# One block of a language model on one core: attention prepared without a barrier, group weights one sequence behind the other

## The reference

```
tok = wte[x];  Q = layernorm(tok) @ W_proj.T;  V = tok @ W_val.T         # 8 heads of 64
traces = decay * (value_traces - erase(Q masked)) + lr * (Q masked)^T V / denom
h = Q shifted by one token @ traces @ W_out.T
x1 = layernorm(h)
q, k, v = x1 @ W_qkv + b_qkv
gw = softmax(gelu(v @ W_gp))                                             # 49 groups a token
group = gw @ gw.T
w = (1 - a) * softmax(q @ k.T * scale * group) + a * group               # a = sigmoid(alpha)
h = h + (w @ v) @ W_proj + b_proj
x2 = layernorm(h)
D, C = softmax over tokens, softmax over slots, of x2 @ phi_n            # 64 experts x 16 slots
h = h + C @ experts(D^T x2)                                              # layernorm, gelu, two layers
```

## Time and profile before

| | us |
|---|---|
| median of 3 runs | 500.75 |
| profiled execution | 499.41 |
| its span | 497.6 |
| PE busy | 450.2 |
| DVE busy | 305.7 |
| ACT busy | 215.2 |
| POOL busy | 145.4 |

### The profile page before, as it was taken

How to read it: one execution, slowest core, us unless ns; L and a number is a source line. 1 busy time by engine, 2 the same in 40 slices (tenths; PEclk the granted TensorE clock), 3 DMA queues, 4 the chain that set the end, 5 groups by cost and what they waited for, 6 DMA issues and landing times.

```text
span 497.6 us, 8397 instructions
## 1 busy us (share of the span) xinstructions
PE 450.2 (90%) x3098; PEld 364.8 (73%) x3098; DVE 305.7 (61%) x829; ACT 215.2 (43%) x398; POOL 145.4 (29%) x235
## 2 busy tenths in 40 slices
PE   5599999799669999999999899999649599999996
PEld 2387756797558888888888788899525387777785
DVE  4689853585844756767775857668522154455475
ACT  2387641399524336644224848163661212112220
POOL 4887400373100262210003930034211221223110
PEclk9999998899879999999999999999978979999999
DMA  8111000003000000400000000027057999997104
GB/s 295 45 42 34 1 2 0 0 2 109 16 0 0 1 1 9 183 1 0 1 0 2 2 0 2 0 88 295 0 200 302 386 345 405 387 375 275 31 27 126
DMA packets 14200, 49.65 MB, mean 100 GB/s; under 512 B 3472, under 2 KB 8496, under 8 KB 9936
## 3 DMA queue, kind: packets, MB, share of 16 engines
q1 hardware_dynamic: 6992, 41.64, 22.0%
q10 hardware_dynamic: 4256, 4.10, 2.4%
q0 software_dynamic: 2912, 3.37, 2.4%
HBM read 45.94 MB, written 3.15 MB: 99 GB/s over the span
## 4 chain that ended last, share of the span: by engine, by line
PE 75%; DVE 7%; ACT 6%; DMA 5%; POOL 4%; issue 3%; ACTq 0%; POOLq 0%; DVEq 0%
PE ps L1053 10%; PE ps L864 9%; PE ps L910 6%; PE ps L1005 4%; PE ps L1030 3%; PE ps L846 2%; PE ps L1041 2%; PE ps L677 2%; DMA ys<-ys_dram 2%; PE ps L890 2%; ACT ec L1271 2%; PE ps L819 2%; PE ps L582 2%; PE ps L893 1%; PE ps L891 1%
## 5 line engine op out<-in xcount | busy, mean ns | idle before, releaser
L1053 PE MATMUL ps<-ys,ct 128*128 128x192 f32 x256 | 52.0, 357 | 5.1 <-DMA ys<-ys_dram 5.1
L1793 DVE SCALAR_TENSOR_TENSOR res<-ps,riC,res 128x192 f32<-128x192 f32 x128 | 46.7, 413 | 12.1 <-PE ps L1053 9.6
L1053 PEld LDWEIGHTS ps<-ys,ct 128*128 128x128 f32 x256 | 41.5, 197 | 15.0 <-issue 8.5
L864 PE MATMUL ps<-pr,et 128*128 128x192 f32 x256 | 46.4, 332 | 2.1 <-DVE et L1641 1.6
L864 PEld LDWEIGHTS ps<-pr,et 128*128 128x128 f32 x256 | 41.1, 189 | 5.2 <-ACT et L1249 3.1
L485 POOL TENSOR_SCALAR ve<-mv 128x1 f32<-128x1 f32 x32 | 12.9, 403 | 103.5 <-DVE mv L1656 61.4
L1354 ACT ACTIVATE hs<-ps 128x384 f32<-128x384 f32 x16 | 7.9, 491 | 79.9 <-PE ps L1005 79.9
L570 POOL DMA_DIRECT2D ys<-ys_dram x32 | 19.7, 619 | 73.9 <-DMA ys_dram<-ysb 68.1
L1238 ACT ACTIVATE scs<-ps,pr 128x1024 f32<-128x1024 f32 x16 | 17.9, 1117 | 41.1 <-PE ps L823 41.1
L1784 DVE COPY ysb<-ps 128x192 f32<-128x192 f32 x16 | 5.7, 358 | 46.8 <-PE ps L1030 46.8
L1242 ACT ACTIVATE zz<-zz,nmx 128x1024 f32<-128x1024 f32 x16 | 18.4, 1150 | 26.4 <-DVE nmx L1635 26.3
(11 more groups left out here) (323 smaller groups left out, 1197.6 us busy)
## 6 DMA issues: line engine op xcount, KB each, us to landing
w1r<-in_p_w SPq DMA_DIRECT2D x16, 1152.0 KB, 11.8
w2r<-in_p_w SPq DMA_DIRECT2D x16, 1152.0 KB, 9.2
ys_dram<-ysb ACTq DMA_DIRECT2D x16, 96.0 KB, 7.7
ys<-ys_dram POOLq DMA_DIRECT2D x32, 48.0 KB, 6.9
phT<-in_p_phi SPq DMA_DIRECT2D x1, 1024.0 KB, 4.8
wT<-in_p_qkv ACTq DMA_DIRECT2D x1, 774.0 KB
out<-res SPq DMA_DIRECT2D x4, 192.0 KB, 3.2
out<-res ACTq DMA_DIRECT2D x4, 192.0 KB, 3.9
```

The lines of the kernel that those rows point to most:

```text
L864: last = mm(d[:, 0:D], et[:, k, :], pr[:, b * KT + k, 0:D], start=(k == 0), stop=(k == KT - 1))
L1053: mm(bank(5 + q % 3)[:, 0:D], ct[:, u % 2, k, :], ys[:, t % YR, b, :], start=True, stop=True).then_inc(m["yp_filled"], 1)
L1793: v.scalar_tensor_tensor(res[:, i, :], bank(5 + q % 3)[:, 0:D], riC[:, i:i + 1], res[:, i, :], ALU.mult, ALU.add).then_inc(m["yp_taken"], 1)
```

## The change

It has these parts:

- The first barrier is gone from all five engines; the waits on tile counts that are needed in its place are added. The tiles in SBUF are laid out in another order, so that what is loaded or written early lies on nothing still in use.
- The loads of wT, wpg, wvT, vt, woT and wpn move to SP's queue, behind the statistics of tile 1. phT and lnT load after the first mixed tile, the other two constants after the last value projection. GpSimd gathers three tiles instead of four ahead of the first factors, and factors 1 and 2 come ahead of gather 4.
- ScalarE loads its first table with a one-element Copy, and the Gelu table with a one-element Gelu, ahead of where they are first needed.
- The beta products of the four head pairs move from the start to right ahead of kB2, where VectorE copies them.
- The key bias is one more column of the k preparations and lies in column 0 of pr; four small products, bks and its scaling go.
- The order of SETUP is now beta, kA, kB1, kB2, nB2, nB1, nA, vA, vB1, vB2. The v preparations run inside the mixed/value loop, in steps 0, 1 and 3.
- The last gram products run right after the first loop's last steps, ahead of the update.
- Gelu, shift, Exp and normalising run for one sequence at a time, those of sequence 0 in part inside the mixed/value loop. scores(0) wait for the transposed group weights of sequence 0 only; sums and transposes of sequence 1 run in step 1 of attention, ahead of turn(0).
- Square and sum of phi are one step later.

```diff
@@ SyncE
+            sp.wait_ge(m["front_stats"], 2)
+            sp.dma_start(wT[:], a["p_qkv"]).then_inc(m["in_attn"], 16)
+            sp.dma_start(wpg[:], a["p_wpg"]).then_inc(m["in_attn"], 16)
...
-            meet(sp, 1)
+            sp.wait_ge(m["h_filled"], 1)
             sp.dma_start(phT[:], a["p_phi"]).then_inc(m["in_phi"], 16)
@@ GpSimd
-            for g in range(4):
+            for g in range(3):
                 gather(g)
             front_factors(0, 1)
+            gather(3)
+            front_factors(1, 3)
             gather(4)
-            front_factors(1, 3)
...
-            meet(pool, 1)
             nc.gpsimd.memset(gw[:], 0.0).then_inc(m["half_ready"], 1)
@@ TensorE, set-up
-            prepare("kB2", at["kA"] + 1)
+            prepare("kA", 1)
...
-            grams(NT - 1)
-            prepare("vA", 0)
...
-            prepare("vB1", at["kB2"] + 1)
+            prepare("kB1", 0)
...
-            prepare("vB2", at["vA"] + 1)
+            pe.wait_ge(m["setup_taken"], at["kA"] + 1)
+            beta_of_pairs()
+            prepare("kB2", at["kA"] + 1)
             pe.wait_ge(m["mm_ready"], 2)
+            pe.wait_ge(m["setup_taken"], at["kB2"] + 1)
@@ TensorE, mixed/value loop and attention
                 if s < NT:
                     mixed(s)
+                if s == 0:
+                    prepare("vA", 0)
+                if s == 1:
+                    prepare("vB1", 0)
                 if 3 <= s < NT + 3:
                     x1_T(s - 3)
+                if s == 3:
+                    prepare("vB2", at["vA"] + 1)
...
-            meet(pe, 1)
+            for j in range(2 * QPS - 2):        # QPS = 4 query blocks a sequence
+                query(j)
+            for j in range(GTS):                # GTS = 2 blocks of gw a sequence
+                gw_T(j)
+            for j in range(2 * QPS - 2, 2 * QPS):
+                query(j)
...
-                if s == 0:
-                    beside_scores()
+                if s == 1:
+                    sums(0)
+                    for j in range(GTS, NB * GTS):
+                        gw_T(j)
+                    sums(1)
@@ ScalarE
+            sc.activation(aw[:, 1:2], ones[:, 0:1], ACT.Gelu)
             for s in range(NT + 6):
+                if s in (1, 2, 4):
+                    round_v({1: "vA", 2: "vB1", 4: "vB2"}[s])
+                if s == KT + 6:
+                    act.wait_ge(m["pr_taken"], KT)
+                    gelu_groups(0)
...
-            meet(act, 1)
-            logit = pr[:, :, D:D + G]
-            sc.activation(logit, logit, ACT.Gelu).then_inc(m["g_gelu"], 1)
+            act.wait_ge(m["pr_taken"], NT)
+            gelu_groups(1)
+            exp_groups(0)
+            sc.activation(aw[:, 1:2], aw[:, 0:1], ACT.Exp, scale=-1.0).then_inc(m["alpha_exp"], 1)
+            for j in range(QPS):
+                query_hi(j)
+            exp_groups(1)
+            for j in range(QPS, 2 * QPS - 2):
+                query_hi(j)
+            for j in range(GTS):
+                gw_hi(j)
+            for j in range(2 * QPS - 2, 2 * QPS):
+                query_hi(j)
@@ VectorE
             for s in range(NT + 4):
+                if s in (1, 2, 4):
+                    round_v({1: "vA", 2: "vB1", 4: "vB2"}[s])
+                if s == KT + 7:
+                    shift_groups(0)
...
-            meet(dve, 1)
+            norm_groups(0)
             for j in range(2):
                 q_lo(j)
+            shift_groups(1)
+            for j in range(2, QPS):
+                q_lo(j)
+            norm_groups(1)
+            for j in range(QPS, 2 * QPS - 2):
+                q_lo(j)
+            for j in range(GTS):
+                gw_lo(j)
+            for j in range(2 * QPS - 2, 2 * QPS):
+                q_lo(j)
...
             for s in range(NT + 1):
+                if s == 1:
+                    u_take(0)
+                    for j in range(GTS, NB * GTS):
+                        gw_lo(j)
+                    u_take(1)
                 if s >= 1:
                     weight(s - 1)
```

More of the change, by code:

```diff
@@ L193, in build @@
         fac = sb("fac", [P, NT, HEADS], where=front)
+        wT = sb("wT", [P, 3, 2, PC], where=front)
+        wTq, wTk, wTv = (wT[:, y] for y in range(3))
+        wpg = sb("wpg", [P, 2, D + G], where=front)
         wpn = sb("wpn", [P, HP, PC], where=front)
@@ L201, in build @@
         cc = sb("cc", [P, 2, D], where=front)
+        cols = sb("cols", [P, 9 + NT + D], where=front)
+        gamA, gamB, gamR = (cols[:, c:c + 1] for c in range(3))
+        betA, betB = cols[:, 3:5], cols[0:DB, 5:7]
+        valid, bproj = cols[:, 9:9 + NT], cols[:, 9 + NT:9 + NT + D]
+        XH = sb("XH", [P, 2, NB * SLOTS * Q], F32R, front)
+        XL = sb("XL", [P, 2, NB * SLOTS * Q], F32R, front)
+        x1t = sb("x1t", [P, 3, XC], where=front)
         nAh = sb("nAh", [P, D], F32R, front)
@@ L231, in build @@
         prs = sb("prs", [P, 2, NP], where=biases)
-        sb("beyond", [P, W1N + W2C - NE - HID - D - 2 * NT - 4 * NP - 4 * (P + 2 * DB)], where=biases)
-        kAh = sb("kAh", [P, P + 2 * DB], F32R, biases)
-        kAl = sb("kAl", [P, P + 2 * DB], F32R, biases)
-        kB1 = sb("kB1", [P, P + 2 * DB], F32R, biases)
-        kB2 = sb("kB2", [DB + 2, P + 2 * DB], F32R, biases)
+        KV = XC + W2N
+        sb("beyond", [P, W1N + W2C - NE - HID - D - 2 * NT - 4 * NP - 4 * KV], where=biases)
+        kv = [sb(f"kv{part}", [rows, KV], F32R, biases) for part, rows in (("Ah", P), ("Al", P), ("B1", P), ("B2", DB + 2))]
+        kAh, kAl, kB1, kB2 = (t[:, 0:XC] for t in kv)
+        vAh, vAl, vB1, vB2 = (t[:, XC:KV] for t in kv)
         biases.close()
@@ L360, in pass_tiles @@
             return []
-        SETUP = ["beta", "kA", "kB1", "kB2", "vA", "vB1", "vB2", "nB2", "nB1", "nA"]
-        SETUP_BANK = [7, 7, 3, 7, 6, 7, 6, 7, 4, 5]
+        SETUP = ["beta", "kA", "kB1", "kB2", "nB2", "nB1", "nA", "vA", "vB1", "vB2"]
+        SETUP_BANK = [7, 7, 6, 7, 6, 4, 5, 5, 6, 5]
         at = {n: k for k, n in enumerate(SETUP)}
@@ L789, in _, with query @@
-            pe.wait_ge(m["gw_ready"], 1)
-            for j in range(NT // 4):
+            def query(j):
+                blk, c0 = divmod(j, 2)
+                w = slice(P, XC) if c0 else slice(0, P)
+                if j >= 4:
+                    pe.wait_ge(m["qpl_taken"], j - 3)
+                elif j >= 1:
+                    pe.wait_ge(m["pr_taken"], min(NT, NT - 2 + j))
+                d = bank(4 + j % 4)
+                b, n = half_of(blk)
+                mm(d, kAh[:, w], X1H[b][:, 0, n], start=True, stop=False)
+                mm(d, kAl[:, w], X1H[b][:, 0, n], start=False, stop=False)
+                mm(d, kAh[:, w], X1L[b][:, 0, n], start=False, stop=False)
+                mm(d, kB1[:, w], X1H[b][:, 1, n], start=False, stop=False)
+                mm(d, kB2[:, w], X1L[b][0:DB + 2, 1, n], start=False, stop=True).then_inc(m["qp_filled"], 1)
@@ L804, in _, with sums @@
-            pe.wait_ge(m["in_phi"], 16 * 4)
-            pe.wait_ge(m["qpl_taken"], 8)
-            pe.wait_ge(m["gwT_taken"], NT // 4)
-            pe.wait_ge(m["x1l_zeroed"], NB)
+            def sums(b):
+                pe.wait_ge(m["qpl_taken"], 2 * QPS)
+                d = bank(6 + b)[:, 0:D]
+                for k in range(KT):
+                    i = b * KT + k
+                    last = mm(d, gw[:, i, :], pr[:, i, 1:1 + D], start=(k == 0), stop=(k == KT - 1))
+                last.then_inc(m["u_filled"], 1)
@@ L1128, in round_up @@
                 last.then_inc(m["setup_hi"], 1)
             def round_k(name):
-                round_up(name, (SCALE, SCALE, SCALE), kAh, kB1, kB2, XC)
+                Ah, _, B1, B2 = (t[:, 0:XC + 1] for t in kv)
+                round_up(name, (SCALE, SCALE, SCALE), Ah, B1, B2, XC + 1)
             def round_v(name):
-                round_up(name, (1.0, 1.0, 1.0), vAh, vB1, vB2, W2N)
+                Ah, _, B1, B2 = (t[:, XC + 1:KV] for t in kv)
+                round_up(name, (1.0, 1.0, 1.0), Ah, B1, B2, D + G)
@@ L1174, in _ @@
             last.then_inc(m["update_taken"], 1)
-            round_v("vA")
-            round_v("vB1")
+            round_k("kB1")
             act.wait_ge(m["mix_done"], 1)
@@ L1416, in round_off @@
                 if part == "A":
-                    last = remainder(Al[:], d[:, 0:n], scale[0], Ah[:])
+                    last = remainder(Al, d[:, 0:n], scale[0], Ah)
                 elif part == "B1":
```

279 lines of the change are left out of this document (132 added, 147 removed).

## The result

| | before | after |
|---|---|---|
| median of 4 runs each, same chip | 500.18 us (499.4 to 500.93) | 509.50 us (507.16 to 510.95) |
| profiled execution | 499.41 | 510.95 |
| its span | 497.6 | 509.1 |

The changed kernel takes 1.018 times as long (95% interval 1.013 to 1.023), 9.3 us more where 2.4 less was forecast, and lies outside the range of 494.5 to 501.6. The profiled execution of the changed kernel is one of the two slowest of its four, so its rows add up to some 2 us more than the medians differ by.

The account below looks back on a forecast made before the run. TensorE, busy 450.2 us (90% of the span), was taken as the bound. Start -0.5, serial stretch -1.7, mixed/value loop +3.3, attention's preparation -3.8, phi +0.3 gave -2.4 us: 497.0 profiled, 498.3 median, range 494.5 to 501.6.

Parts of the forecast that it names:

- The first loop: 22 to 66 us: pace stays 2.85 us a tile; three small VectorE operations make the weighing 0.25 us late.
- the five rivals: Alternative outcomes: clock holds 496.1; gain given back 499.7; slower 501.6; slower table switch 499.6; barrier without effect, 0.9 slower.
- the signs by which the prediction would call itself wrong: Value projections ending before 118 us, or turn(0) less than 29 or more than 34 us behind them.
- The start: 0 to 22 us: masked tile 0 at 19.3 instead of 20.25; between 1.0 gained and 0.5 lost, 0.5 gain taken.
- The serial stretch: 66 to 92 us: v preparations leave, beta pairs and a 1.55 wait come; 1.7 us gained, between 0.4 and 2.2.
- Rival 3: New waits ahead of n products and turn(0) each bring the clock down; 0.9 us slower, 501.6; chance 0.12.
- The mixed/value loop: v preparations and sequence 0's group work delay GpSimd: 2.2 and 1.1 us lost, loop 3.3 longer (2.0 to 4.5).
- The preparation of attention: Value projections to turn(0): 31.5 us against 35.3, 3.8 gained (2 to 5.5), with low clock ahead of scores(0).
- rival 1: Clock holds ahead of scores(0) and a late gather costs nothing: 4.6 us gained, 496.1; chance 0.20.
- Phi: In attention, sums over squared phi one tile later: scaling 2 us late, costing TensorE 0.3 us, between 0 and 1.
- The table: ScalarE's table switch in attention's preparation: load of 1.28 us counted, without the skill's 1.38 drain.
- rival 4: Slower table switch: ScalarE stands another 1.28 us before the first Exp; 1.1 us gained, 499.6; chance 0.03.

Follow-up runs that it names:

- e1: The changed kernel with VectorE's statistics taken one tile further ahead again (four tiles ahead); 501.45 us, 1.005 of the kernel before.
- e2: The kernel before with only the statistics taken one tile later (three ahead); 506.97 us, 1.016 of the kernel before.
- e10: The changed kernel, statistics still three ahead, GpSimd's factors taken for single tiles instead of pairs; 499.50 us, 0.999 of the kernel before.
- e5: e1 with gather 4 ahead of factors 1 and 2, statistics of tile 2 ahead of beta rows, late loads held until tile 6's statistics; 498.20 us.
- e13: The same kernel as e6, profiled again; 496.89 us, 0.993 of the kernel before.
- e14: Kernel with start, pairs, kB2 wait, turn(0) and attention's preparation reworked on e1, plus Gelu and shift of sequence 0 later in the mixed/value loop; 483.87 us.
- e15: e14 with the first v preparation (vA) moved ahead of mixed tile 0; 482.69 us, 0.965 of the kernel before.
- e6: e1 with the beta products of the head pairs back at the start, the n products' wait for kB2 kept; 497.69 us, 0.993 of the kernel before.
- e4: e1 with the beta products of the head pairs and kB2 put right behind kB1; 503.19 us, 1.005 of the kernel before.
- e7: e1 with sequence 1's gw transposes ahead of both sums, and the wait for u moved from turn(0) to attend(i); 498.02 us, 0.996 of before.

## Why the prediction was wrong, step by step

- **The first loop: the step that failed.** The prediction has it that the first loop "keeps its pace of 2.85 us a tile". It counted three small VectorE operations that move to the loop's end and took the rest as unchanged. It measured 10.5 us more, and e1, e2 and e10 give nearly all of it to the statistics taken one tile later against factors taken in pairs. How far one engine runs ahead of another has no instruction and so no row of its own; the step had only counted instructions. None of the five rivals looked at the loop either, and neither of the signs by which the prediction would call itself wrong came: the value projections ended at 133.04, not before 118, and turn(0) came 31.65 us behind them.
- **The start: right mechanism, wrong size.** Gather 4 went out at 13.68 (13.4 forecast), and VectorE stood until its rows were there at 19.60, 5.9 us later. The step gave this gather 3.9 us before it delays anything and said that 6.3 would cost 1.4; by its own numbers that is 2.4. With 2.0 for the 5.9 measured, 19.3 becomes 21.3, against 21.55. So the bound was a microsecond too tight, and the value taken from between the bounds was on the wrong side. e5 shows what its three edits are worth together: 4.1 us up to masked tile 0, 3.2 up to the weighing.
- **The serial stretch: each part near, the clock missing.** The pairs took 2.5 us instead of 2.05 (90.71 to 93.21, eight times 0.31), the wait 1.62 instead of 1.55. The 2.05 halved the old 0.51 of a pair as "cold", but the clock column reads 1.00 beside those pairs, so no row bore out the halving. 26.69 for 25.47 forecast: the n products, 2.4 us slower at clock 0.50, are more than the difference. Rival 3 forecast slow n products and a slow attend(0), and both came. Its mechanism, a fall brought by the wait, is borne out at attend(0) only. At the n products the clock fell 0.2 us before the wait began, in e1 1.2 us before, and in e13 it held through the same wait. What makes it fall there stays open.
- **The mixed/value loop: right.** 3.0 us more for 3.3, with waits of GpSimd where the two named parts are: 1.85 us behind the v preparations (2.2 forecast) and 1.56 behind the group work (1.1). One part was forecast too large and the other too small, so the near sum is in part luck. The experiments bear out 1.7 of the 3.0 (e14 0.95, e15 0.8); the rest is read from the waits.
- **The preparation of attention: right.** From the end of the value projections (133.04) to turn(0) it is 31.65 us for 31.5, to scores(0) 15.0 for 14.95, and behind the idle of 3.83 us the clock reads 0.50 from 149 to 152 us as forecast; rival 1 fell. The idle ahead of turn(0) is 1.97 for 1.9. That the clock also fell behind it and attend(0) took 4.51 us instead of 2.87 is rival 3. The barrier's removal does what it says: the first query starts 0.11 us behind the start of the last value product.
- **Phi: right in kind.** VectorE's scaling waits 1.95 us for GpSimd's power (2 forecast), and nothing of that can be seen on TensorE.
- **The table.** In the changed kernel's trace the switch to Exp is a load of 1.28 us at 134.02, with Exp at 135.31. The rule of the Trainium skill (ScalarE: Activation LUTs, What ACT_TABLE_LOAD costs) that a switch also costs a drain of 1.38 us isn't borne out here either, as the Exp starts where the load ends: rival 4 fell.
- **Sum.** 1.3 + 10.5 - 0.7 + 3.0 - 3.6 + 1.7 = 12.2 us up to turn(1) (12.14 unrounded), of which the span shows 11.5 and the medians 9.3. Without the loop's loss it is e1: 0.5% (0.2 to 0.8) slower than before, not the 2.4 us faster of the forecast. Up to turn(1) e1's trace is 5.0 us behind the forecast's course: 1.9 from the start, 0.5 from the loop, 1.2 from the serial stretch, 1.4 between turn(0) and turn(1), small amounts in the rest. That e1's 501.45 lies at rival 3's 501.6 is luck, since that rival had neither the start nor the loop in its sum.

## What to carry to other kernels

When a diff changes how many tiles ahead one engine runs, draw the ring of waits through all engines and count its steps, even if no instruction is added: here one tile less against factors in pairs cost 10.5 us, more than all the rest. The ring showed in the profile as every engine less busy at once, with short waits that name each other in turn. A reordering for an engine that waits is best judged by how late its first dependant on the bounding engine is: three such reorderings (gather 4 ahead of the factors with earlier statistics and later loads, transposes ahead of the sums, sequence 1's work behind scores(0)) brought 3.3, 3.4 and 3.8 us, and with them the version without the barrier runs in 482.7 us, 3.5% (3.2 to 3.7) below the kernel before.

## What the runs showed of the hardware

- The granted clock of TensorE fell to 0.50 in a stretch in which TensorE stood nowhere (e6, 75 to 81 us, products of 64 to 257 columns), and held at 1.00 in the same kernel through a wait of 1.44 us (e13). Executions of one kernel differed in this, by 7.2 us in that stretch. A wait next to a fall is thus no proof that it caused it: in five of the seven executions with the pairs in the serial stretch the clock was at 0.50 before the wait began (after, e1, e4, e7, e10). Ahead of turn(0) the fall did go with the wait, in eight executions of nine.
- A gather beside large loads took 5.9 us in the changed kernel (gather 4, issued at 13.68, its rows taken at 19.60) and 6.3 before, where 2.7 is the median, whether the loads went out ahead of the first gathers or, from 9.76 on, ahead of the fifth.
